# Layer one's experts: the second bias spread over the partitions at load and added by VectorE, instead of one-row products on TensorE

## The chip, the cores and the metric

One core of a Trainium2 chip runs the whole program. The metric is the device time of one execution in microseconds (us): the median of several runs, and for the profiled execution its own time. A profile holds one execution, with the start and duration of nearly every instruction of the five engines: PE (TensorE; its weight loads are listed apart as PEld), DVE (VectorE), ACT (ScalarE), POOL (GpSimd) and SP (SyncE), which here only issues DMA transfers.

## The reference, cut to what matters

The program is a model of four layers on an input of 8 sequences x 256 tokens x 128 channels. Each layer has an attention part and a feed-forward part. The change touches the feed-forward part of layer one only (`L0_ffn` in the reference, `l0_ffn` in the kernel): an attention, then four experts, of which each token takes the one with the largest logit.

```python
def moe(x, gate_w, gate_b, W1, b1, W2, b2):
    logits = x @ gate_w.T + gate_b
    top = jnp.argmax(logits, axis=-1)
    onehot = jax.nn.one_hot(top, N_EXPERTS, dtype=x.dtype)      # 4 experts
    h = jax.nn.relu(jnp.einsum('btd,ehd->bteh', x, W1) + b1)    # 128 -> 512
    y = jnp.einsum('bteh,edh->bted', h, W2) + b2                # 512 -> 128
    return jnp.einsum('bted,bte->btd', y, onehot)
...
h = _layernorm(x, axis=-1) * (1 + cb) + sb
x = x + gb * _L0_ffn_ref(h, ...)
```

`b2` has 4 x 128 numbers: one row of 128 for each expert. Everything is fp32.

## The kernel before

The kernel is written out by hand, engine by engine, with semaphores between them. Layer one runs as one pipeline over 16 places `m`: 0 to 7 are the attention of the 8 sequences, 8 to 15 (`is_ffn(m)`) the feed-forward parts of the same 8. A sequence is two tiles of 128 tokens (`T` = 2, index `t`). In iteration `m` the engines work on the scores of place `m+1`, the weighing of place `m`, the projections of place `m+3` and, where place `m-1` is a feed-forward part, on its experts. The order on each engine is that of the code.

An iteration on PE has two stretches. The *attention stretch* is six rounds `k` of scores, masks and weighing (L1376 to L1410), in which PE, DVE (a max over every round's scores, L2296), ACT (exponentials, L3377) and POOL take turns; the stacks that the scores read are put together by small transfers that SP issues (`expand_half`, L598), 24 for each place. The *expert stretch* follows (L1411 to L1423): `turn_post`, `rise` of experts 0 and 1, `choose_expert`, then `fall` 0, `rise` 2, `fall` 1, `rise` 3, `fall` 2, `fall` 3. `rise(m, e)` makes the four 128-wide pieces of an expert's hidden layer (L1345, ACT adds `b1` and takes the relu, L3429). `fall(m, e)` multiplies by `W2` (L1361, four products for each token tile, summed in PSUM) and adds `b2` with a fifth product (L1362), whose weight operand is one row of ones and whose moving operand is one row of 128 biases.

Every fp32 product stands in the profile as two records of PE, so that `fall` shows 8 records of L1361 and 2 of L1362 for a token tile.

DVE picks the expert of every token (`pick_expert`, L2208 to L2226, a mask `picks` of 0 and 1), then for each expert waits for `fall` and adds bank x mask to the sequence's rows in SBUF (`add_expert`, L2232, one instruction for each token tile), and at the end multiplies by the gate and adds to `x` (`finish_ffn`, L2238 and L2241). `fall` 2 and 3 write the PSUM banks of `fall` 0 and 1 and wait until `add_expert` has read these.

The weights of a part are one matrix of 128 rows in HBM, in which `b2` fills only row 0 (512 columns, the other rows are zeros). SP loads the matrix with one transfer (`load`, L651) into one of two regions of SBUF; PE waits for that of `l0_ffn` in `scale_of_ffn` (L1117), at the beginning of the program.

Of the kernel before, what the change touches and what calls it, by code (L numbers as in the profile page):

```python
# [9 lines left out]
ALU = mybir.AluOpType  # L10
# [3 lines left out]
P = 128  # L14
B, S, D = 8, 256, 128
T = S // P
# [12 lines left out]
E0, C0 = 4, 4  # L29
# [29 lines left out]
WEIGHED = PHASES[:-1]  # L59
# [28 lines left out]
def offsets(cols):  # L88
    at, out = 0, {}
    for name, n in cols:  # L90
        out[name] = (at, n)
        at += n
    return out, at
# [29 lines left out]
H_RING = 6  # L123
# [15 lines left out]
def is_ffn(m):  # L139
    return B <= m < 2 * B  # L140
# [11 lines left out]
def last_of(m):  # L152
    return 2 * B - 1 if m < 2 * B else 3 * B - 1
# [17 lines left out]
def adaln_program(nc, x_in, c_in, const_in, ali_in, weights_in, out):  # L171
    ctx = ExitStack()
    with ctx:
        def sb(name, shape, dt=F32):
            return ctx.enter_context(nc.sbuf_tensor(name, shape, dt))
# [8 lines left out]
        def once(name):  # L184
            return ctx.enter_context(nc.semaphore(name))
# [13 lines left out]
        places = {ph: offsets(COLUMNS[ph]) for ph in WEIGHED}  # L199
        region = [sb(f"weights{i}", [P, max(places[ph][1] for ph in WEIGHED[i::2])]) for i in range(2)]  # L200

        def W(ph, name, rows=P):
            at, n = places[ph][0][name]
            return region[WEIGHED.index(ph) % 2][0:rows, at:at + n]
# [3 lines left out]
        ones = sb("ones", [P, P])  # L208
# [42 lines left out]
        hid = sb("hid", [P, 2, C0, T * P])  # L251
# [107 lines left out]
        h_ring = tail[1][:, 0:H_RING * S].rearrange("p (i t d) -> p i t d", t=T, d=D)  # L359
# [66 lines left out]
        loaded = [once(f"weights_loaded_{ph}") for ph in WEIGHED]  # L426
# [161 lines left out]
        def there(n):  # L588

            return 0 <= n < N3  # L590
# [56 lines left out]
        def _(sp):  # L647
            sp.dma_start(x[:], x_in.rearrange("b (t p) d -> p (b t) d", p=P)).then_inc(x_loaded, 16)
            def load(i):
                n = DOWN_AT if WEIGHED[i] == "l1_ffn" else places[WEIGHED[i]][1]  # L650
                sp.dma_start(region[i % 2][:, 0:n], weights_in[WEIGHED[i]][:, 0:n]).then_inc(loaded[i], 16)  # L651

            load(0)
            sp.dma_start(silu_c[:], c_in).then_inc(c_loaded, 16)
# [6 lines left out]
            for i in range(HPG):  # L661
                at = 64 * i + STACK_ROWS
# [45 lines left out]
            for i, ph in enumerate(WEIGHED):  # L708
                if 1 <= i < len(WEIGHED) - 1:

                    sp.wait_ge(pass_done.sem, pass_done(ph, 0, 1))
                    if ph == "l1_ffn":
                        n = places[ph][1]
# [346 lines left out]
        def _(pe):  # L1060
            mm = nc.tensor.matmul
# [48 lines left out]
            def spread_mod(ph, j, to):  # L1110
                for b in range(B):
                    last = mm(to[:, b * D:(b + 1) * D], silu_n[:, b, :], W(ph, "wmod")[:, j * D:(j + 1) * D], start=True, stop=True)
                last.then_inc(mod_psum, 1)

            def scale_of_ffn(ph="l0_ffn"):

                pe.wait_ge(loaded[1], 16)  # L1117
                pe.wait_ge(mod_taken, 2)
                spread_mod(ph, 1, scored)

# [227 lines left out]
            def fall(m, e, ph="l0_ffn"):  # L1348
                pe.wait_ge(relu_done.sem, relu_done(m, 2 * e + 2))
                if e < 2:  # L1350
                    if m + 1 <= last_of(m):
                        pe.wait_ge(weighed_taken.sem, weighed_taken(m + 1, e + 1))
                    if is_ffn(m - 1):
                        pe.wait_ge(fall_used.sem, fall_used(m - 1, e + 3))
                else:
                    pe.wait_ge(fall_used.sem, fall_used(m, e - 1))
                for t in range(T):
                    o = pb[4 + e % 2][:, t * D:(t + 1) * D]
                    for c in range(C0):
                        at = (e * C0 + c) * D  # L1360
                        mm(o, hid[:, e % 2, c, t * P:(t + 1) * P], W(ph, "w2")[:, at:at + D], start=c == 0, stop=False)  # L1361
                    last = mm(o, ones[0:1, :], W(ph, "b2", 1)[:, e * D:(e + 1) * D], start=False, stop=True)  # L1362
                last.then_inc(fall_psum.sem, 1)

            def piped(ph):
# [535 lines left out]
        def _(dve):  # L1901
            V_ = nc.vector
# [197 lines left out]
            def link(ins):  # L2100
                linked[0] += 1
                ins.then_inc(link_dve, 1)

            def linkup():

                dve.wait_ge(link_dve, linked[0])
# [101 lines left out]
            picks = small[8][:, 0:T * E0].rearrange("p (t e) -> p t e", t=T)  # L2208

            def pick_expert(m, ph="l0_ffn"):  # L2210
# [14 lines left out]
                link(V_.tensor_tensor(picks, order, every_e, ALU.is_equal))  # L2225
                linkup()  # L2226

            def add_expert(m, e):
                h = h_ring[:, m % H_RING]
                dve.wait_ge(fall_psum.sem, fall_psum(m, e + 1))  # L2230
                for t in range(T):
                    last = V_.scalar_tensor_tensor(h[:, t, :], pb[4 + e % 2][:, t * D:(t + 1) * D], picks[:, t, e:e + 1], h[:, t, :], ALU.mult, ALU.add)  # L2232
                last.then_inc(fall_used.sem, 1)
                dve.wait_ge(fall_used.sem, fall_used(m, e + 1))
# [115 lines left out]
            def piped(ph):  # L2350
                first = RUNS[ph][0]
                if ph == "l2_attn":
                    dve.wait_ge(pass_done.sem, pass_done(ph, 0, 1))
                    V_.memset(stacks[0], 0.0).then_inc(stacks_clear, 1)
                    V_.memset(stacks[1], 0.0).then_inc(stacks_clear, 1)
                    V_.memset(ones_h, 1.0).then_inc(stacks_clear, 1)
                stats_piped(first)
                mod_piped(ph)
                stats_piped(first + 1)
                norm_piped(first)  # L2360
                stats_piped(first + 2)
                if ph == "l0_attn":
                    dve.wait_ge(ali_loaded, 16 * HPG * 2)
                    V_.tensor_copy(stacks[0].rearrange("p g side n -> p (g side n)"), staging).then_inc(stacks_clear, 1)
                intake_piped(first)
                norm_piped(first + 1)
                stats_piped(first + 3)
                gates_piped(gates_attn, MODS[ph] + 2, MODS[ph] + 2, scored)
                intake_piped(first + 1)
                norm_piped(first + 2)  # L2370
                stats_piped(first + 4)
                if ph == "l0_attn":
                    scale_of_ffn()
                intake_piped(first + 2)
                if ph == "l0_attn":
                    mod_ffn()
                for m, there in iterations(ph):
                    for k in range(NU):
                        if m in (3 * B - 1, 3 * B) and k in (0, 3):
                            (wide_norm_of if k else wide_stats_of)("l2_ffn", m - 3 * B + 1)  # L2380
                        if k == 1 and there(2) and is_ffn(m + 2):
                            keys_ffn(m + 2)
                        if k == 2 and there(-1):
                            tokens_piped(m - 1)
                        if m >= first and k == 3 and there(3):
                            if is_ffn(m + 3):
                                queries_ffn(m + 3)
                            else:
                                intake_piped(m + 3)
                        if k == 4 and there(-1):  # L2390
                            if is_ffn(m - 1):
                                post_stats(m - 1)
                            else:
                                result_piped(m - 1)
                        if k == 5 and there(1):
                            values_piped(m + 1)
                        if k == 5 and there(3) and is_ffn(m + 3):
                            latent_stats(m + 3)
                        if there(1):
                            max_piped(m + 1, k)  # L2400
                        if m >= first and k == 0 and there(3):
                            if is_ffn(m + 3):
                                rms_ffn(m + 3)
                            else:
                                norm_piped(m + 3)
                        if k == 3 and there(4) and is_ffn(m + 4):
                            norm_ffn(m + 4)
                        if k == 5 and there(3) and is_ffn(m + 3):
                            latent_norm(m + 3)
                        if k == 5 and there(-1) and is_ffn(m - 1):  # L2410
                            post_norm(m - 1)
                    if there(-1) and is_ffn(m - 1):
                        pick_expert(m - 1)
                        for e in range(E0):
                            add_expert(m - 1, e)
                        finish_ffn(m - 1)
                    if m >= first and there(5):
                        stats_piped(m + 5)
# [1448 lines left out]
```

## Time and profile before

| | us |
|---|---|
| median of 3 runs | 2461.11 |
| lowest and highest run | 2457.08, 2466.51 |
| profiled execution, its own time | 2468.3 |
| profiled execution, span from first to last instruction | 2466.3 |
| PE busy in the span | 1913.0 |
| DVE busy in the span | 1691.8 |

The span is what the rows of the trace add up to; 2.0 us lie around it. Busy time is a sum over the whole program. Layer one's pipeline takes the first 551 us of the span, the experts stand between 248 and 551 us.

### The profile page before, as it was taken

The numbers are of one execution on the slowest core, as the hardware profiler recorded it, in microseconds if no ns is written. First come the engines' busy times: TensorE is split into PE (matmuls) and PEld (weight loads), VectorE is DVE, ScalarE is ACT, GpSimd is POOL, SyncE is SP. The second block draws the span as 40 slices with busy tenths as digits, with TensorE's granted clock in tenths as the row PEclk, the third lists the DMA queues.
The fourth block names the chain that finished last, engine by engine and source line by source line (L and its number), as shares of the span: only waits on it lengthen the run. The fifth ranks groups of instructions, "written<-read, shape, count | busy, mean of one in ns | idle before, by whom it ended". The sixth has DMA issues, their size and how long they took to land.

```text
span 2466.3 us, 43977 instructions
## 1 busy us (share of the span) xinstructions
PE 1913.0 (78%) x14818; PEld 1352.5 (55%) x14818; DVE 1691.8 (69%) x5219; ACT 1136.3 (46%) x3338; POOL 902.0 (37%) x1198
## 2 busy tenths in 40 slices
PE   5888888985266676676669999999587679999955
PEld 3545666662155565564557566666354347677742
DVE  6777344326588888878976866666675458888647
ACT  2533333325777677777632222222154237666620
POOL 3433121005185467447543000000441127767711
PEclk8977889885555555555556999999698689999967
DMA  4111001002000000000001000000210100000000
GB/s 126 47 42 40 19 15 35 5 18 89 14 7 7 14 9 13 8 14 1 1 1 49 1 1 0 0 0 0 52 48 26 65 12 1 2 1 2 1 1 17
DMA packets 57809, 49.61 MB, mean 20 GB/s; under 512 B 7048, under 2 KB 55912, under 8 KB 57064
## 3 DMA queue, kind: packets, MB, share of 16 engines
q1 hardware_dynamic: 54548, 45.53, 5.8%
q8 instruction: 108, 1.77, 0.3%
q10 hardware_dynamic: 3040, 1.38, 0.2%
q14 instruction: 113, 0.93, 0.1%
HBM read 19.78 MB, written 1.05 MB: 8 GB/s over the span
## 4 chain that ended last, share of the span: by engine, by line
PE 38%; DVE 30%; SPq 10%; issue 8%; ACT 8%; POOL 6%; DMA 1%; DVEq 0%; ACTq 0%; POOLq 0%
SPq L598 9%; PE bank L1628 5%; PE bank L1620 5%; PE bank L1621 5%; DVE weights L2658 4%; ACT rope_c L3534 3%; ACT rope_s L3534 3%; PE bank L1345 3%; PE bank L1361 2%; PE bank L1712 2%; DVE small L2696 2%; DVE feat_o L2708 2%; DVE nmax L2585 1%; PE bank L1531 1%; PE bank L1761 1%
## 5 line engine op out<-in xcount | busy, mean ns | idle before, releaser
L1531 PE MATMUL bank<-V,probsT 128*128 128x9 f32 x1024 | 234.8, 362 | 79.1 <-ACT probsT L3545 79.1
L1531 PEld LDWEIGHTS bank<-V,probsT 128*128 128x128 f32 x1024 | 224.9, 327 | 116.1 <-ACT probsT L3545 96.7
L2296 DVE TENSOR_REDUCE nmax<-bank 128x4 f32<-128x1024 f32 x144 | 176.0, 1222 | 87.2 <-PE bank L1158 87.0
L3600 ACT ACTIVATE hid<-bank 128x512 f32<-128x512 f32 x144 | 85.7, 597 | 277.3 <-PE bank L1621 268.4
L1628 PEld LDWEIGHTS bank<-weights,hid 128*128 128x128 f32 x1152 | 149.9, 191 | 74.9 <-issue 64.1
L2903 DVE TENSOR_TENSOR hid<-hid,bank 128x512 f32<-128x512 f32 x144 | 98.6, 687 | 117.0 <-PE bank L1628 113.7
L3545 ACT ACTIVATE probsT<-bank 128x512 f32<-128x512 f32 x128 | 76.1, 597 | 179.5 <-PE bank L1518 177.1
L1628 PE MATMUL bank<-weights,hid 128*128 128x128 f32 x1152 | 151.9, 275 | 7.8 <-DVE O L2917 5.1
L1620 PE MATMUL bank<-O,weights 128*128 128x512 f32 x288 | 149.3, 600 | 0.9 <-DMA weights<-in_weights_l_ffn 0.9
L864 POOL MEMSET big<- 128x4096 bf16 x1 | 3.5, 3512 | 398.1 <-DVE x L2943 398.1
L1621 PE MATMUL bank<-O,weights 128*128 128x512 f32 x288 | 148.1, 596 | 0.0
L3634 ACT ACTIVATE big<-bank,nmax 128x256 f32<-128x256 f32 x256 | 119.7, 485 | 51.9 <-DVE nmax L3078 51.9
L754 POOL TENSOR_TENSOR big<-big,rinv 128x512 f32<-128x512 f32 x128 | 132.8, 1052 | 19.1 <-DVE rinv L3084 19.1
L2917 DVE SCALAR_TENSOR_TENSOR O<-bank,O 128x128 f32<-128x128 f32 x496 | 138.9, 342 | 0.0
L3377 ACT ACTIVATE feat_o<-bank 128x1024 f32<-128x1024 f32 x72 | 73.7, 1024 | 115.6 <-PE bank L1187 87.7
L3377 ACT ACTIVATE O<-bank 128x1024 f32<-128x1024 f32 x72 | 73.7, 1024 | 115.3 <-PE bank L1187 87.5
L2585 DVE TENSOR_REDUCE nmax<-bank 128x2 f32<-128x512 f32 x128 | 84.8, 682 | 35.0 <-PE bank L1505 35.0
L1505 PE MATMUL bank<-qT 48*128 48x256 bf16 x256 | 70.3, 402 | 45.7 <-ACT weights L3488 33.3
L3078 DVE TENSOR_REDUCE nmax<-bank 128x2 f32<-128x512 f32 x128 | 81.8, 680 | 24.5 <-PE bank L1712 24.5
L1621 PEld LDWEIGHTS bank<-O,weights 128*128 128x128 f32 x288 | 55.3, 192 | 69.9 <-issue 69.9
L3429 ACT ACTIVATE hid<-bank,weights 128x256 f32<-128x256 f32 x128 | 52.9, 471 | 80.2 <-PE bank L1345 80.1
L1518 PE MATMUL bank<-const,big 128*128 128x128 f32 x256 | 61.6, 420 | 36.2 <-POOL big L970 36.2
(677 smaller groups left out, 5404.0 us busy)
## 6 DMA issues: line engine op xcount, KB each, us to landing
qT<-parts SPq DMA_DIRECT2D x276, 32.0 KB
big<-V SPq DMA_DIRECT2D x192, 32.0 KB
big<-parts SPq DMA_DIRECT2D x180, 32.0 KB
weights<-in_weights_l_ffn SPq DMA_DIRECT2D x1, 4832.0 KB, 15.3
weights<-in_weights_l_attn SPq DMA_DIRECT2D x1, 3904.0 KB, 12.0
weights<-in_weights_l_ffn SPq DMA_DIRECT2D x1, 3628.0 KB, 14.6
qT<-V SPq DMA_DIRECT2D x96, 32.0 KB
weights<-in_weights_l_ffn SPq DMA_DIRECT2D x1, 2304.0 KB, 8.6
```

The costliest lines, as they stand in the source:

```text
L598: queue.dma_start(stacks[m % STACKS][to, u * HALF:(u + 1) * HALF], pair_of(m, at, *of)).then_inc(stack_in[u].sem, 16)
L754: nc.gpsimd.tensor_tensor(row, row, rinv[:, h % H, :].unsqueeze(2).to_broadcast([P, T, S]), ALU.mult).then_inc(scaled.sem, 1)
L1531: last = mm(pb[1][:, t * S + h * wide:t * S + (h + 1) * wide], probsT[:, h % 2, at:at + P], values_of(b, k)[:, h * wide:(h + 1) * wide], s ...
L1620: mm(pb[two][:], W(ph, "gate")[:, cols], pair_feat, start=True, stop=True)
L1621: mm(pb[two + 1][:], W(ph, "up")[:, cols], pair_feat, start=True, stop=True).then_inc(hid_psum.sem, 1)
L1628: last = mm(pb[6 + e % 2][:, j * D:(j + 1) * D], risen(e)[:, j * P:(j + 1) * P], W(ph, "down")[:, e * D:(e + 1) * D], start=True, stop=True)
L2296: V_.tensor_reduce(to, scored.rearrange("p (i a n) -> p i a n", i=HPG, n=n), AX.X, ALU.max, negate=True).then_inc(score_max.sem, 1)
L2585: V_.tensor_reduce(nmax[:, h, :], tiles(pb[2 + n % 3]), AX.X, ALU.max, negate=True).then_inc(max_ready.sem, 1)
L2917: last = V_.scalar_tensor_tensor(pair_sum[:, j, :], down[:, j, :], w, pair_sum[:, j, :], ALU.mult, ALU.add)
L3377: nc.scalar.activation(turned_probs[n % TURNS], turned_scores, ACT.Exp).then_inc(turned_exp.sem, 1)
L3534: nc.scalar.activation(signs[signed[0] % len(signs)], row_of(b, j), ACT.Sign, bias=tried[at][:, 0, j:j + 1], scale=-1.0, accum_out=tried[a ...
L3634: last = nc.scalar.activation(probs3[h % PROBS3][:, t * S:(t + 1) * S], pb[h % 4][:, t * S:(t + 1) * S], ACT.Exp, bias=nmax[:, h % H, t:t ...
```

## The change

The sum of five products in `fall` becomes one of four: L1362 goes. The biases are spread over all 128 partitions when the weights are loaded: the load of `l0_ffn` becomes three transfers, the columns ahead of `b2`, the columns behind it, and row 0 of the `b2` columns read once for each partition. DVE adds the bias times the mask in SBUF (`add_bias`, two instructions for each expert), for experts 0 and 1 ahead of `add_expert` 0, for experts 2 and 3 ahead of `add_expert` 1. Each `add_bias` ends with a wait for its own instructions (`linkup`).

```diff
             def load(i):
                 n = DOWN_AT if WEIGHED[i] == "l1_ffn" else places[WEIGHED[i]][1]
-                sp.dma_start(region[i % 2][:, 0:n], weights_in[WEIGHED[i]][:, 0:n]).then_inc(loaded[i], 16)
+                if WEIGHED[i] == "l0_ffn":
+                    at, n_bias = places["l0_ffn"][0]["b2"]
+                    end = at + n_bias
+                    sp.dma_start(region[1][:, 0:at], weights_in["l0_ffn"][:, 0:at]).then_inc(loaded[i], 16)
+                    sp.dma_start(region[1][:, end:n], weights_in["l0_ffn"][:, end:n]).then_inc(loaded[i], 16)
+                    sp.dma_start(region[1][:, at:end], weights_in["l0_ffn"][0:1, at:end].to_broadcast([P, n_bias])).then_inc(loaded[i], 16)
+                else:
+                    sp.dma_start(region[i % 2][:, 0:n], weights_in[WEIGHED[i]][:, 0:n]).then_inc(loaded[i], 16)
...
             def scale_of_ffn(ph="l0_ffn"):
-                pe.wait_ge(loaded[1], 16)
+                pe.wait_ge(loaded[1], 3 * 16)
...
                     for c in range(C0):
                         at = (e * C0 + c) * D
-                        mm(o, hid[:, e % 2, c, t * P:(t + 1) * P], W(ph, "w2")[:, at:at + D], start=c == 0, stop=False)
-                    last = mm(o, ones[0:1, :], W(ph, "b2", 1)[:, e * D:(e + 1) * D], start=False, stop=True)
+                        last = mm(o, hid[:, e % 2, c, t * P:(t + 1) * P], W(ph, "w2")[:, at:at + D], start=c == 0, stop=c == C0 - 1)
                 last.then_inc(fall_psum.sem, 1)
...
+            def add_bias(m, e, ph="l0_ffn"):
+                h = h_ring[:, m % H_RING]
+                for t in range(T):
+                    link(V_.scalar_tensor_tensor(h[:, t, :], W(ph, "b2")[:, e * D:(e + 1) * D], picks[:, t, e:e + 1], h[:, t, :], ALU.mult, ALU.add))
+                linkup()
...
                         for e in range(E0):
+                            if e < 2:
+                                add_bias(m - 1, 2 * e)
+                                add_bias(m - 1, 2 * e + 1)
                             add_expert(m - 1, e)
```

What stands on PE in the expert stretch of the first feed-forward place, from `choose_expert` to the first scores of the next iteration, before (a product is one row here, and equal rows are counted):

```order
L1329 MATMUL bank<-weights,next_feat 128x4 x2
L1361 MATMUL bank<-weights,hid 128x128 x4
L1362 MATMUL bank<-weights,ones 128x128
L1361 MATMUL bank<-weights,hid 128x128 x4
L1362 MATMUL bank<-weights,ones 128x128
L1345 MATMUL bank<-next_feat,weights 128x256 x4
```

And in the changed kernel, where `choose_expert` is L1336, `fall` L1368 and `rise` L1352:

```order
L1336 MATMUL bank<-weights,next_feat 128x4 x2
L1368 MATMUL bank<-weights,hid 128x128 x8
L1352 MATMUL bank<-next_feat,weights 128x256 x4
L1368 MATMUL bank<-weights,hid 128x128 x8
L1352 MATMUL bank<-next_feat,weights 128x256 x4
L1368 MATMUL bank<-weights,hid 128x128 x16
L1186 MATMUL bank<-big 128x256 x4
```

Eight one-row products go from each of the eight expert stretches; nothing else changes its place on PE. On DVE the same stretch, from the end of `pick_expert` to the next statistics, before:

```order
L2225 TENSOR_TENSOR small<-small 128x8
L2232 SCALAR_TENSOR_TENSOR weights<-bank,small,weights 128x128 x8
L2238 TENSOR_TENSOR weights<-weights 128x256
L2241 TENSOR_TENSOR x<-x,weights 128x256
L2112 BN_STATS stats<-x 128x6 x2
```

And in the changed kernel, where `add_bias` is L2237 and `add_expert` L2244:

```order
L2231 TENSOR_TENSOR small<-small 128x8
L2237 SCALAR_TENSOR_TENSOR weights<-weights,small 128x128 x4
L2244 SCALAR_TENSOR_TENSOR weights<-bank,small,weights 128x128 x2
L2237 SCALAR_TENSOR_TENSOR weights<-weights,small 128x128 x4
L2244 SCALAR_TENSOR_TENSOR weights<-bank,small,weights 128x128 x6
L2250 TENSOR_TENSOR weights<-weights 128x256
L2253 TENSOR_TENSOR x<-x,weights 128x256
L2118 BN_STATS stats<-x 128x6 x2
```

Eight additions in SBUF come in, four ahead of the first `add_expert` and four ahead of the second. On SP the queue of the program's first microseconds in the changed kernel, where the one transfer of 7256 columns has become three:

```order
L670 DMA big<-in_ali 6x4096 x2
L672 DMA big<-probs 3x8x256 x2
L654 DMA weights<-in_weights_l_ffn 128x5720
L655 DMA weights<-in_weights_l_ffn 128x1024
L656 DMA weights<-in_weights_l_ffn 128x512
L598 DMA qT<-parts 8x4x512
```

Their place in the queue is that of the single transfer, ahead of the first stack's transfers.

## Rows read from the trace of the kernel before

**Rows 1.** The page: span, busy time of each engine, granted clock in 40 slices

```profile
span 2466.3 us, 43977 instructions
PE 1913.0 (78%) x14818; PEld 1352.5 (55%) x14818; DVE 1691.8 (69%) x5219; ACT 1136.3 (46%) x3338; POOL 902.0 (37%) x1198
...
PEclk8977889885555555555556999999698689999967
```

**Rows 2.** Chain that ended last, 384 to 405 us: start, us, what

```profile
387.47 1.00 PE bank L1361 x8
388.47 0.41 PE bank L1362 x2
...
390.38 1.92 PE bank L1345 x8
...
399.84 1.09 PE bank L1361 x8
...
402.43 0.43 PE bank L1362 x2
...
402.95 0.62 DVE weights L2232 x2
```

**Rows 3.** The same chain, 254 to 552 us: shares, two of the longest pieces

```profile
by line: PE bank L1345 20.2%; PE bank L1361 19.3%; issue 16.6%; PE bank L1362 7.8%; PE bank L1207 3.4%; DVE nmax L2296 3.1%; DVE stats L2112 1.8%; PE bank L1315 1.5%; PE bank L1179 1.4%; DVE weights L2232 1.2%; ACT next_feat L3418 1.2%; PE 
...
293.76 3.78 PE bank L1345 x8
...
420.29 31.79 issue
```

**Rows 4.** Line L1362: duration in ns (min/median/max), starts, and who waited

```profile
L1362 PEld LDWEIGHTS bank<-weights,ones x128: 181/182/184, 256.2 to 549.4; 1*128 1x128 f32 x128
L1362 PE MATMUL bank<-weights,ones x128: 270/321/372, 256.2 to 549.5; 1*128 1x128 f32 x128
...
  DVE weights L2232: 99.7, 32
```

**Rows 5.** Line L1361: duration in ns (min/median/max), first and last start

```profile
L1361 PEld LDWEIGHTS bank<-weights,hid x512: 186/192/192, 255.1 to 549.0; 128*128 128x128 f32 x171
```

**Rows 6.** Timeline 388 to 397 us, ACT and DVE: start, us, idle before

```profile
388.50 0.17 DVE L2225 TENSOR_TENSOR small<-small 128x8 f32<-128x8 f32 x1
...
390.49 0.61 DVE L2232 SCALAR_TENSOR_TENSOR weights<-bank,small,weights 128x128 f32<-128x128 f32 x2 [1.82 <-PE bank L1362]
...
395.22 0.61 DVE L2232 SCALAR_TENSOR_TENSOR weights<-bank,small,weights 128x128 f32<-128x128 f32 x2 [4.12 <-PE bank L1362]
396.27 1.64 ACT L3429 ACTIVATE hid<-bank,weights 128x256 f32<-128x256 f32 x4 [3.09 <-PE bank L1345]
```

**Rows 7.** Groups of DVE by form: busy us, mean ns, idle before

```profile
L2232 DVE SCALAR_TENSOR_TENSOR weights<-bank,small,weights 128x128 f32<-128x128 f32 x64 | 19.5, 346 | 99.7 <-PE bank L1362 99.7
L1971 DVE SCALAR_TENSOR_TENSOR probs<-gate_sign,next_gate_b 128x128 f32<-128x128 f32 x8 | 2.3, 293 | 0.3
```

**Rows 8.** Timeline of SP, 340 to 420 us

```profile
370.98 18.08 SPq L598 DMA_DIRECT2D big<-parts  x24
```

**Rows 9.** Timeline, transfer page and chain of the first 30 us

```profile
8.71 0.42 SPq L651 DMA_DIRECT2D weights<-in_weights_l_ffn  x1
...
26.27 3.75 PE L1112 MATMUL bank<-weights,feat_o 128*128 128x128 f32 x16 [0.35 <-DVE weights L2267]
...
weights<-in_weights_l_ffn SPq DMA_DIRECT2D x1, 3628.0 KB, 14.6
...
out<-x SPq DMA_DIRECT2D x4, 256.0 KB, 2.3
...
24.00 0.74 SPq L598
```

**Rows 10.** Windows: PE, PEld, DVE, ACT, POOL busy, granted clock, DMA share, GB/s

```profile
294.00:300.00 6.00, 6.00 (x28) 4.15 (x29) 0.00 (x0) 2.06 (x5) 0.00 (x0) 0.51 0.13 38
300.00:318.00 18.00, 18.00 (x132) 15.22 (x131) 3.81 (x15) 5.24 (x13) 0.00 (x0) 1.00 0.00 1
...
384.00:404.00 20.00, 20.00 (x151) 16.65 (x151) 3.83 (x15) 6.48 (x16) 0.00 (x0) 0.97 0.05 15
```

## The prediction, made before the changed kernel ran

> **What bounds the kernel now.** I read the page first, then the line that goes, then the chain that ended last around it, and only then the neighbours on the other engines. The page [rows 1] says that PE is the busiest engine with 1913.0 of 2466.3 us, but a share over the whole program proves nothing for one stage. So the next question is who waits for the line that goes. The view of L1362 shows that DVE's `add_expert` (L2232) waited for it 32 times, 99.7 us in all [rows 4]: 8 sequences x 4 experts, every one. DVE is ahead of PE in the whole expert stretch. The view also gives the places: 128 records from 256.2 to 549.5 us, that is 64 products, 8 in each of 8 sequences.
>
> The chain that ended last then shows whether PE's time there sets the end. In the stretch of one sequence it runs through PE without a break: 1.00 us of L1361, 0.41 of L1362, again and again, with `rise` (1.92 us) between, up to the last bias product at 402.43, behind which stands DVE's last `add_expert` at 402.95 [rows 2]. From 254 to 552 us L1362 has 7.8% of the chain, 23.2 of 298 us [rows 3]. One piece of 31.79 us beginning at 420.29 is an "issue" with nothing in it; PE worked there on the experts of another sequence, so the chain lost its way in that sequence and 23.2 us belong to seven, 3.3 us each. PE is the bound in all eight expert stretches, and its windows say the same: 18.00 of 18.00 and 20.00 of 20.00 us busy [rows 10].
>
> **What goes.** 64 products. The price of one is what PE's order loses by it, start to start: 0.41 us (two records) [rows 2]. This is not its listed duration (a median of 321 ns a record [rows 4]), because durations overlap. It is also not the price of a normal product: eight records of L1361 take 1.09 us, 0.136 each, a bias record 0.205. 64 x 0.41 = 26.2 us; from the chain's shares, 8 x 3.3 = 26.5. I take 26.2.
>
> Whether a price of 0.41 really disappears is the one doubt on PE's side. The weight loads of the two kinds last nearly the same, 182 ns with one row and 192 ns with 128 rows [rows 4, 5]. The Trainium skill (TensorE: Matmul & The Clock Gate, section on LDWEIGHTS) says that a load of few rows takes as long as a full one, since the columns count; the loads of this trace agree. Read as a rule for the whole product, a bias product would cost like any other, and that is a rival below. The starts speak for 0.41: they are what follows it that is late, and without it the next group of L1361 can begin where the bias product began.
>
> **What is added on DVE.** 64 instructions on 128x128 in SBUF, one-to-one with the products. This form (bias, mask column and sum all in SBUF) isn't in the trace. The nearest rows: 293 ns for the same operation with SBUF operands and a constant, and 346 ns for the same with one operand in PSUM [rows 7]; a pair of the latter lasts 0.61 to 0.62 us [rows 2, 6]. So 18.8 to 22.1 us more of DVE's time. I take the upper end, 0.62 a pair. Are they hidden? In the sequence shown the mask is ready at 388.50 + 0.17 = 388.67 [rows 6]. Two pairs end at 389.91, with two short waits about 390.0. `fall` 0 loses two bias products, so `add_expert` 0 could begin at 390.49 - 0.82 = 389.67: it begins 0.3 us late and ends at about 390.6. That costs nothing, since its only customer is `fall` 2, which began two groups of 1.50 us ahead of 399.84 [rows 2], at 396.8, and begins after the change 4 x 0.41 sooner, at 395.2. The other two pairs, 1.24 us, stand ahead of `add_expert` 1, before which DVE sat idle for 4.12 us [rows 6], of which 0.8 us go because PE is sooner (only the two bias products of `fall` 1 lie between) and 0.3 us to the late start: 3.0 us remain for 1.24. From there to the last `add_expert`, which is the one on the chain, DVE has nothing new. Cost on the path 0; if the cover were gone, 32 pairs x 0.62 = 19.8 us.
>
> **What is late next in the stretch.** PE sooner means ACT's relu may become the wait. The tightest is expert 3: its relu runs 396.27 to 397.91 [rows 6] and moves ahead by 4 x 0.41 = 1.64 us with `rise` 3, to an end of 396.3. `fall` 3 stood at 399.84 [rows 2] and moves by 6 x 0.41 to 397.4. 1.1 us of room; no wait.
>
> **What is late next behind it.** The next attention stretch begins 8 x 0.41 = 3.3 us sooner. Its scores need the stack that SP puts together. SP's 24 transfers run 370.98 to 389.06 [rows 8] and land within 2 or 3 us (an estimate, from the 2.3 us in which a 256 KB transfer lands [rows 9]); they are wanted when the experts' last product ends at 402.9 [rows 2], after the change at 399.6. 8 us of room. SP, POOL and ACT all start each round from something that PE or DVE did after the expert stretch, so they move with it. At the last sequence DVE's `finish_ffn` releases layer two, which begins sooner by the same amount.
>
> **The load.** Two transfers more: two more issues of 0.42 us, and SP has nothing to do between 9.13 and 24.00 [rows 9]. The bytes are the same (3628 KB). Before, they landed at 8.71 + 14.6 = 23.3 us; the first reader on PE ran at 26.27 and was released by DVE, not by the load [rows 9]. A read of one row by 128 partitions isn't in the trace. Bounds: 0, as the bytes are no more, and 2.3 us, as for a transfer of 256 KB by itself, plus 0.84 for the issues; that is 26.4 at worst, 0.2 us past PE's start. Besides, from 24.00 us on the chain is SP's own queue [rows 9], not PE. I take 0.
>
> **Sum.** -26.2 on PE, 0 elsewhere. The profiled execution would go from 2468.3 to 2442.1 us (span 2466.3 to 2440.1). It stands 7.2 us above the median of the runs, 2461.1, so the median goes to 2434.9, -1.06%. A change of less than about 0.5% (12.3 us) couldn't be told from none; this one can.
>
> **Rivals.**
> *The bias product is worth less.* If removing it gives only a normal product's time, 2 x 0.136 = 0.27 us, since the rest of the 0.41 is something that the next group pays anyway, the gain is 64 x 0.27 = 17.5 us: 2443.6. For it: the equal loads. Against it: every start-to-start row. The Trainium skill's rule on loads (TensorE: Matmul & The Clock Gate, LDWEIGHTS), read for the whole product, would give this time.
> *DVE's additions land on the path.* All 32 pairs uncovered leave 26.2 - 19.8 = 6.4 us: 2454.7. Against it: the idle times [rows 6], with 3.0 us for 1.24 at one place and 4.6 us to spare at the other.
> *The head start is swallowed in the attention stretch*, by the stack's transfers or a wait that isn't tied to PE: 2461. It needs SP to end 8 us later than it does.
> *The granted clock (the one that ends on the other side).* `rise` 0 runs at the 1.2 GHz level (3.78 us for eight records at 293.76, clock 0.51 from 294 to 300), the rest of the stretch at 2.4 GHz (1.92 us, clock 1.00) [rows 2, 3, 10]. When the level rises isn't in the program's hands. If with the changed rhythm it rose only after `fall` 0, `rise` 2 and `fall` 1 (2.2 + 1.9 + 2.2 = 6.3 us at the high level), each sequence would lose 6.3 us: 50.4 - 26.2 = +24.2, 2485. It decides from 3.3 us a sequence on, and is measurable as slower from 4.8. Against it: before these products PE is as busy as ever, and they go from the middle of a stretch without an idle microsecond. In small doses (a group or two of 1.9 us won or lost in some sequences) it belongs to the range of the forecast.
>
> **How the numbers follow.** The forecast has 0.82, the cheaper product 0.09, DVE on the path 0.03, swallowed 0.04, the clock 0.02. The likeliest case is 2435. Its own spread: the runs before lie 4 to 5 us around their median, and two or three groups of 1.9 us of clock go either way, so 2426 to 2444. The range of 8 in 10 reaches on to the cheaper product with 3 us of spread: 2425 to 2447. Faster by over 0.5% (below 2448.8) are the forecast and the cheaper product: 0.91. Within 0.5%: DVE on the path and swallowed, 0.07. Slower: the clock, 0.02.
>
> **What would show it.** The timeline of a sequence: the two groups of `fall` are 1.09 us apart instead of 1.50, `fall` lasts 2.2 us instead of 3.0, and from the first `fall` to the next scores pass 12.1 us instead of 15.4. `add_bias` shows about 300 to 346 ns an instruction, and DVE's idle time ahead of `add_expert` falls from 99.7 us by some 20 (its own new work) and 26 (PE is sooner), to about 53; only at expert 0 is it nil. The three transfers land before 26.3 us and no wait for them stands on PE. From 254 us on the eight sequences come sooner by 3.3 us each, and behind 551 us everything has the old distances. Wrong would be: distances of 1.2 us instead of 1.09 between groups, a wait of PE for L2244 in `fall` 2, or windows of the expert stretch with a clock below 0.9.

## The result, and the profile after

| | before | changed |
|---|---|---|
| median, us | 2461.11 | 2424.7 |
| lowest and highest run | 2457.08, 2466.51 | 2418.24, 2427.16 |
| span of the profiled execution | 2466.3 | 2425.1 |
| PE busy | 1913.0 | 1862.2 |
| DVE busy | 1691.8 | 1713.8 |

The ratio is 0.9846, with a 95% interval of 0.9829 to 0.9863: the changed kernel is 36.4 us faster. In a second set of runs it was 2425.06 against 2460.64 us, a ratio of 0.9858 (0.9842 to 0.9874). The forecast was 2435 us, a gain of 26; the time lies 0.3 us below the range. The direction and the place were right, the gain was 1.4 times as large as forecast.

The page of the changed kernel:

```profile
span 2425.1 us, 43787 instructions
PE 1862.2 (77%) x14690; PEld 1323.2 (55%) x14690; DVE 1713.8 (71%) x5283; ACT 1136.0 (47%) x3338; POOL 902.6 (37%) x1198
...
PEclk7987889965555555555557999999698789999967
```

PE is busy for 50.8 us less, more than the 26 that the forecast took off it; DVE for 22.0 us more, the upper bound of the forecast (22.1). The mean granted clock over the program is the same (0.768 and 0.769).

The chain that ended last through the experts of one sequence (start, us, what), to be read beside [rows 2]; in this kernel `rise` is L1352, `choose_expert` L1336, `fall` L1368, `add_expert` L2244:

```profile
372.90 0.34 PE bank L1336 x4
373.24 1.89 PE bank L1368 x16
375.13 1.73 PE bank L1352 x8
376.86 1.78 PE bank L1368 x16
378.64 1.73 PE bank L1352 x8
380.37 3.58 PE bank L1368 x32
...
384.05 0.62 DVE weights L2244 x2
```

The products of two token tiles (16 records) take 1.78 us, 0.89 for the eight that took 1.09 before, and `rise` takes 1.73 us where it took 1.92 [rows 2]. So not only the bias products are gone; what stood behind them became faster. The chain of the kernel before has both times for the same eight records, 0.89 us behind `rise` and 1.09 behind a bias product:

```profile
392.31 0.89 PE bank L1361 x8
393.20 0.41 PE bank L1362 x2
393.61 1.09 PE bank L1361 x8
```

The stretch from the first `fall` to the beginning of `finish_ffn` shows the gain in one number. The windows view of that stretch, in the kernel before and in the changed one (us, then busy time and count of PE, PEld, DVE, ACT, POOL, granted clock, DMA share, GB/s):

```profile
387.33:403.60 16.27, 16.27 (x122) 13.67 (x121) 3.43 (x15) 3.97 (x10) 0.00 (x0) 1.00 0.03 9
```

```profile
373.10:384.69 11.59, 11.59 (x106) 10.80 (x105) 5.88 (x22) 3.96 (x10) 0.00 (x0) 1.00 0.03 8
```

PE is busy without a break in both, at the 2.4 GHz level (granted clock 1.00) in both; the stretch is 4.68 us shorter. It is as long in each of the eight sequences (16.26 to 16.27 before, 11.59 to 11.60 after), which makes 37.4 us. `rise` 0 and 1 ahead of it are 1.4 us longer in sum (51.0 against 52.4), and the attention stretches (from 228 us on) 4.1 us shorter (141.4 against 137.3). In both the granted clock wanders from sequence to sequence and from execution to execution (0.57 to 1.00). Over the thirteen kernels profiled here, whose code in these two places is the same, the sums were 135.2 to 141.4 us and 48.5 to 52.6 us. These differences are no effect of the change that a run here could show.

DVE and the additions in the same sequence (timeline):

```profile
374.27 0.17 DVE L2231 TENSOR_TENSOR small<-small 128x8 f32<-128x8 f32 x1
374.48 1.26 DVE L2237 SCALAR_TENSOR_TENSOR weights<-weights,small 128x128 f32<-128x128 f32 x4
375.78 0.61 DVE L2244 SCALAR_TENSOR_TENSOR weights<-bank,small,weights 128x128 f32<-128x128 f32 x2
376.42 1.26 DVE L2237 SCALAR_TENSOR_TENSOR weights<-weights,small 128x128 f32<-128x128 f32 x4
378.75 0.61 DVE L2244 SCALAR_TENSOR_TENSOR weights<-bank,small,weights 128x128 f32<-128x128 f32 x2 [1.06 <-PE bank L1368]
```

Beside [rows 6]: `add_expert` 0 finds its product ready and waits for nothing, `add_expert` 1 still waits 1.06 us for PE after four additions. The view of L2244 counts what is left of the 99.7 us of [rows 4]:

```profile
  PE bank L1368: 41.0, 24
```

24 waits instead of 32: the eight of expert 0 are gone, and nothing else is.

### The profile page after: what moved, and what is told of

The parts are those of the page before. It is cut to its first block, busy times and chain, and to the rows that moved or that the text cites. A ratio compares the mean times of both kernels' runs of the same rounds, so it can differ in the third digit from the quotient of the medians.

```text
span 2425.1 us, 43787 instructions
## 1 busy us (share of the span) xinstructions
PE 1862.2 (77%) x14690; PEld 1323.2 (55%) x14690; DVE 1713.8 (71%) x5283; ACT 1136.0 (47%) x3338; POOL 902.6 (37%) x1198
## 4 chain that ended last, share of the span: by engine, by line
PE 39%; DVE 31%; ACT 9%; issue 8%; SPq 6%; POOL 6%; ACTq 1%; DMA 0%; DVEq 0%; POOLq 0%
SPq L598 5%; PE bank L1634 5%; PE bank L1626 5%; PE bank L1627 5%; DVE weights L2673 4%; ACT rope_c L3549 3%; ACT rope_s L3549 3%; PE bank L1352 3%; PE bank L1718 2%; PE bank L1368 2%; DVE small L2711 2%; DVE feat_o L2723 2%; DVE nmax L2308 1%; DVE nmax L2600 1%; PE bank L1537 1%
## 6 DMA issues: line engine op xcount, KB each, us to landing
weights<-in_weights_l_ffn SPq DMA_DIRECT2D x1, 2860.0 KB, 12.1
```

## The experiments

The question was where the 11 us beyond the forecast's 26.2 came from. Theory A: few-row weight operands between full ones break the overlap of weight loads and products at both borders. Here a border is the place where a weight operand of few rows and one of 128 rows follow each other, and a full-row product is one whose operands have all 128 rows. Theory B: a fifth product simply costs 0.58 us (4.68 / 8). The figure to watch is the stretch from the first `fall` to `finish_ffn`, because in none of the kernels it varied by more than 0.02 us over the eight sequences.

**All 128 rows.** Rows 1 to 127 of the bias columns are zeros in HBM, so the product may read them all:

```diff
-                    last = mm(o, ones[0:1, :], W(ph, "b2", 1)[:, e * D:(e + 1) * D], start=False, stop=True)
+                    last = mm(o, ones[0:128, :], W(ph, "b2", 128)[:, e * D:(e + 1) * D], start=False, stop=True)
```

> The kernel before, with the fifth product of `fall` over all 128 rows instead of one (a weight operand of 128 x 128 ones; rows 1 to 127 of the bias columns are zeros, so the sum is the same). Theory A: it is the one-row weight operand between 128-row operands that is dear; it breaks the overlap of weight loads and products at both borders. In the trace of before the group of eight L1361 records takes 0.89 us behind `rise` and 1.09 us behind a bias product, and a record in the long groups of the changed kernel takes 0.112 us. Then a full-row bias product costs 2 x 0.112 = 0.22 us instead of 0.58, `fall` group and bias 1.12 us instead of 1.50, the stretch from the first `fall` to `finish_ffn` 11.59 + 8 x 0.22 = 13.4 us (before 16.27, changed kernel 11.59), and the whole program about 23 us below the kernel before (ratio 0.991). Theory B: a fifth product costs 0.58 us whatever its rows (a product of its own kind, with the ones as operand, or the larger sum): stretch 16.3 us, ratio 1.000.

2438.47 us, ratio 0.9897 (0.9876 to 0.9919), stretch 13.38 us. Theory A expected 13.4, Theory B 16.3: A holds, B falls. The bias products multiply 128 times as many numbers, and the kernel is 23 us faster than the kernel before. Its chain through `fall` 0, `rise` 2 and part of `fall` 1:

```profile
254.68 1.00 PE bank L1361 x8
255.68 0.22 PE bank L1362 x2
255.90 0.89 PE bank L1361 x8
256.80 0.22 PE bank L1362 x2
257.02 1.73 PE bank L1345 x8
258.75 0.89 PE bank L1361 x8
```

The bias product takes 0.22 us instead of 0.41, and what stands behind it 0.89 and 1.73 instead of 1.09 and 1.92 [rows 2].

The timelines show where the time is lost. First the kernel before, at one bias product: the load of its weight operand (PEld) and its product (PE) begin together, and so do the load and the product behind it.

```profile
388.40 0.29 PEld L1362 LDWEIGHTS bank<-weights,ones 1*128 1x128 f32 x2
388.40 0.48 PE L1362 MATMUL bank<-weights,ones 1*128 1x128 f32 x2
388.81 0.30 PEld L1361 LDWEIGHTS bank<-weights,hid 128*128 128x128 f32 x2
388.81 0.38 PE L1361 MATMUL bank<-weights,hid 128*128 128x128 f32 x1
```

Then the kernel with 128 rows, where each load begins 0.1 us ahead of its product, under the product before:

```profile
255.41 0.30 PEld L1362 LDWEIGHTS bank<-weights,ones 128*128 128x128 f32 x2
255.51 0.39 PE L1362 MATMUL bank<-weights,ones 128*128 128x128 f32 x2
255.63 0.64 PEld L1361 LDWEIGHTS bank<-weights,hid 128*128 128x128 f32 x5
255.74 0.61 PE L1361 MATMUL bank<-weights,hid 128*128 128x128 f32 x4
```

So the overlap that Theory A spoke of is broken at both borders. What keeps the load back there no view shows.

**64 rows.** The same edit with 64.

> As the kernel before, with the fifth product of `fall` over 64 rows (row 0 the biases, the others zeros). Theory A says that the loss is in any operand with fewer than 128 rows: stretch from the first `fall` to `finish_ffn` 16.3 us, ratio 1.000, as with one row. A variant of A, by which the loss grows with the missing rows, gives something between: about 14.8 us and 0.995. Theory B: 16.3 us and 1.000, so this run says something only if the full-row run is faster.

2459.81 us, ratio 0.9987 (0.9971 to 1.0003), stretch 16.28 us: no better than one row. The loss doesn't grow with the missing rows. The view of L1362 in this kernel, against that of one row [rows 4], and then of the kernel with 128 rows:

```profile
L1362 PEld LDWEIGHTS bank<-weights,ones x128: 182/184/186, 256.1 to 548.6; 64*128 64x128 f32 x128
L1362 PE MATMUL bank<-weights,ones x128: 272/322/373, 256.1 to 548.7; 64*128 64x128 f32 x128
```

```profile
L1362 PEld LDWEIGHTS bank<-weights,ones x128: 191/192/193, 255.4 to 521.9; 128*128 128x128 f32 x128
L1362 PE MATMUL bank<-weights,ones x128: 274/275/276, 255.5 to 522.0; 128*128 128x128 f32 x128
```

The durations of the loads hardly differ; what differs is the spread of the products, 272 to 373 ns against 274 to 276. One of the two records of a few-row product is 0.1 us longer, about half of what the way in costs (0.19 us, below).

**The two one-row products side by side.**

```diff
                 for t in range(T):
                     o = pb[4 + e % 2][:, t * D:(t + 1) * D]
+                    if t == 1:
+                        mm(o, ones[0:1, :], W(ph, "b2", 1)[:, e * D:(e + 1) * D], start=True, stop=False)
                     for c in range(C0):
                         at = (e * C0 + c) * D
-                        mm(o, hid[:, e % 2, c, t * P:(t + 1) * P], W(ph, "w2")[:, at:at + D], start=c == 0, stop=False)
-                    last = mm(o, ones[0:1, :], W(ph, "b2", 1)[:, e * D:(e + 1) * D], start=False, stop=True)
+                        last = mm(o, hid[:, e % 2, c, t * P:(t + 1) * P], W(ph, "w2")[:, at:at + D], start=c == 0 and t == 0, stop=c == C0 - 1 and t == 1)
+                    if t == 0:
+                        mm(o, ones[0:1, :], W(ph, "b2", 1)[:, e * D:(e + 1) * D], start=False, stop=True)
```

> As the kernel before, but the two one-row products of a `fall` stand next to each other: the first token tile's as its last, the second tile's as its first. Theory A (the loss is at the borders between one row and 128 rows): half the borders go. Two products together cost 4 x 0.112 + one pair of borders 0.36 = 0.81 us instead of 1.17, the stretch falls by 4 x 0.36 = 1.4 us to 14.8, the program by 11.5 us, ratio 0.9953. Theory B (the loss sits in the product itself): nothing changes, stretch 16.3 us, ratio 1.000.

2449.29 us, ratio 0.9939 (0.9919 to 0.9959), stretch 14.92 us. Theory A again: it expected 14.8, because it let four pairs of borders go, though the last way out lies behind the stretch and only seven borders go (7 x 0.193 = 1.35 us). The chain (here the first tile's product is L1365, the second's L1360, the others L1363):

```profile
255.88 1.00 PE bank L1363 x8
256.88 0.41 PE bank L1365 x2
257.29 0.22 PE bank L1360 x2
257.52 1.09 PE bank L1363 x8
258.60 1.73 PE bank L1345 x8
```

The second one-row product costs 0.22 us, the price of a full one. What is dear is not the one row but the change: 0.19 us on the way in (0.41 - 0.22), 0.20 on the way out (1.09 - 0.89). The three stretches give one price. The kernel before has 15 borders inside a stretch (8 in, 7 out, the last way out lies behind it): (16.27 - 13.38) / 15 = 0.193 us. Side by side has 8 borders: 13.38 + 8 x 0.193 = 14.92, as measured. A full-row bias product is (13.38 - 11.59) / 8 = 0.224 us.

**How many rows make a border.** Two runs with 127 and 96 rows, then two with 65 and 32, one profiled execution each; the edit is that of the first experiment with another number.

> As the kernel before, with the fifth product of `fall` over 127 rows (the last row of zeros left out; the sum is the same). If any difference in the number of rows makes the border (Theory A in its plain form), the stretch from the first `fall` to `finish_ffn` is 16.27 us as with 1 and 64 rows. If it is the groups of 32 rows that an operand touches, 127 rows touch all four like 128, and the stretch is 13.38 us.

> As the kernel before, with the fifth product of `fall` over 96 rows, three of the four groups of 32. Both readings of Theory A say 16.27 us for the stretch from the first `fall` to `finish_ffn`; 13.38 would mean that the border lies between 64 and 96 rows.

> As the kernel before, with the fifth product of `fall` over 65 rows. 64 rows gave 16.28 us from the first `fall` to `finish_ffn`, 96 and 127 rows 13.38. If the border lies where an operand no longer fits in 64 rows, this run shows 13.38; if it lies higher (three groups of 32 begun), it shows 13.38 as well, and only if all of 96 rows must be there 16.27.

> As the kernel before, with the fifth product of `fall` over 32 rows. Theory A in its present form (an operand of at most 64 rows beside one of more): 16.27 us from the first `fall` to `finish_ffn`, as with 1 and 64 rows.

| rows of the bias product | stretch, us | time, us |
|---|---|---|
| 1 | 16.27 | 2461.11 (median) |
| 32 | 16.26 to 16.27 | 2456.59 |
| 64 | 16.28 | 2459.81 (median) |
| 65 | 13.38 | 2438.89 |
| 96 | 13.38 | 2434.6 |
| 127 | 13.38 | 2438.44 |
| 128 | 13.38 | 2438.47 (median) |

The expectation for 96 rows was wrong in both its readings, and with it Theory A in its plain form, by which anything short of 128 rows is "few". The limit lies between 64 and 65 rows, and no step shows among 1, 32 and 64 rows or among 65, 96, 127 and 128. For these four kernels the stretch of the one profiled execution decides; it is the same in all eight sequences. The view of L1362 with 65 rows is that of 128:

```profile
L1362 PEld LDWEIGHTS bank<-weights,ones x128: 190/191/192, 256.3 to 522.7; 65*128 65x128 f32 x128
L1362 PE MATMUL bank<-weights,ones x128: 273/274/275, 256.4 to 522.8; 65*128 65x128 f32 x128
```

The Trainium skill says on another page than the one that the prediction weighed (TensorEngine Tiling (Array Packing), Key Properties and Overview) that the array can be split into tiles of 64 or 32 rows for a contract dimension of at most 64, and that changing this mode drains the engine. The limit of 64 rows agrees with these runs. But the kernel names no tiles, and no run shows that the array changes its mode here or that a drain is what passes in those 0.193 us; the runs show their number, where they fall, and that the load doesn't begin ahead of its product there.

**Without DVE's additions.** The second bias is left out.

```diff
-                            if e < 2:
-                                add_bias(m - 1, 2 * e)
-                                add_bias(m - 1, 2 * e + 1)
                             add_expert(m - 1, e)
```

> The changed kernel without `add_bias`: the second bias is left out altogether. Theory of the prediction: DVE's 64 additions are hidden behind PE, so the stretch from the first `fall` to `finish_ffn` stays at 11.6 us and the time is that of the changed kernel, ratio to before 0.9846 within its interval. Rival: they delay something after all (the late `add_expert` of expert 0 holds up `fall` 2): then this run is up to 8 x 1.2 = 10 us faster than the changed kernel, ratio 0.981.

2420.49 us, ratio 0.9829 (0.9809 to 0.9848), against 0.9846 (0.9829 to 0.9863) and 0.9858 (0.9842 to 0.9874) with the additions. The intervals overlap, but this one also takes in the rival's 0.981, so the times alone don't decide. The stretch does: the rival's late `fall` 2 would lengthen it, and it is 11.59 to 11.60 us in every sequence, as with the additions. They cost nothing there. Of the 5.6 us between this profiled execution and that of the changed kernel in its second set, 3.6 lie in `rise` 0 and 1 (48.6 us against 52.2), at clocks that wander in all kernels: two kernels without any addition had 52.6 and 48.5 us there (64 and 32 rows). The view of L2244 shows the cover that the additions took up, 62.3 us of waits against 41.0:

```profile
  PE bank L1368: 62.3, 32
```

**The additions behind the last `add_expert`.** `add_bias` for all four experts directly ahead of `finish_ffn`, where nothing covers it.

> The changed kernel with all four `add_bias` behind the last `add_expert`, where DVE's work stands on the chain. Eight additions and their waits take 2.52 us in the changed kernel's trace (1.26 + 1.26). If what hides them is only their place ahead of `fall`'s end, the stretch from the first `fall` to the first scores' max grows by 2.5 us in each of 8 sequences: 20 us above the changed kernel, about 2445, ratio to before 0.993. If DVE has slack in the following attention stretch as well, less than half of that is seen.

2443.29 us, ratio 0.9925 (0.9908 to 0.9942): 18.2 us above the changed kernel in the same set of runs. The stretch is 14.19 to 14.20 us, 2.6 longer, 20.8 in all. The timeline:

```profile
266.15 0.61 DVE L2244 SCALAR_TENSOR_TENSOR weights<-bank,small,weights 128x128 f32<-128x128 f32 x2 [1.18 <-PE bank L1368]
266.80 2.56 DVE L2237 SCALAR_TENSOR_TENSOR weights<-weights,small 128x128 f32<-128x128 f32 x8
269.40 0.42 DVE L2250 TENSOR_TENSOR weights<-weights 128x256 f32<-128x256 f32 x1
```

The same 64 instructions cost 0 or about 20 us by where they stand. Half of the change's gain hangs on that place.

**The load by itself.** The kernel before with the three transfers in place of the one, and nothing else.

> The kernel before with the load of `l0_ffn` as three transfers and everything else as it was. All theories of the prediction: nothing is gained or lost, ratio 1.000, the first stack's transfers of SP start at 24 us as before, and no wait of PE or DVE for the three transfers. Rival, from the changed kernel's trace, in which the sixth stack's transfers begin 2.9 us sooner (210.22 against 213.16) before any expert ran: the three transfers shorten the start, ratio 0.999.

2458.06 us, ratio 0.9992 (0.9981 to 1.0004), stretch 16.26 to 16.27 us. Neither a gain nor a loss that could be told from none. In the trace of the changed kernel the last of the three was issued at 9.60 us and took 14.1 us to land:

```profile
weights<-in_weights_l_ffn SPq DMA_DIRECT2D x1, 256.0 KB, 14.1
```

It landed at 23.7 us, 0.4 later than the single transfer of before [rows 9] and ahead of PE's first reader, which ran at 26.02 us in the changed kernel.

**The changed kernel once more.**

> The changed kernel once more, beside the two others on the same chip. Theory A (a one-row product between 128-row products costs 0.58 us: 0.22 of its own and 0.19 at each border): 64 x 0.58 = 37.4 us less than before, 2424, ratio 0.985, and the stretch from the first `fall` to `finish_ffn` 11.59 us in every sequence. Rival (the gain beyond 26 us is luck of the granted clock): a ratio nearer 0.989 in fresh runs.

2425.06 us, ratio 0.9858 (0.9842 to 0.9874), stretch 11.59 to 11.60. The gain beyond 26 us was no luck of one set: 0.989, the ratio of the forecast's gain, lies outside both intervals.

## Why the prediction was right or wrong

**PE bounds all eight expert stretches:** right. From the first `fall` to the last PE has no idle time in either kernel, in any of the eight sequences.

**The price of a bias product:** this is the step that failed, as a term of the sum that was mis-sized. The prediction said "The starts speak for 0.41: they are what follows it that is late, and without it the next group of L1361 can begin where the bias product began." The next group does begin there, but it isn't the same group: behind a bias product it took 1.09 us, behind another full product it takes 0.89. A bias product's 0.41 us were 0.22 of its own and 0.19 of border, and 0.19 more stood on the account of its successor. Its whole price inside a stretch was 8 x 0.224 + 15 x 0.193 = 4.69 us for a sequence, 37.5 for eight, against 26.2 forecast and 37.4 found. The rows for it were in the trace of before: in the chain of [rows 2], in lines that it left out, eight records of L1361 took 0.89 us where they stood behind `rise`. The prediction used the 1.09 as the natural pace of such a product ("0.136 each") and so never asked why two groups of one line differ. It even put `fall` 2 at 396.8, "two groups of 1.50 us ahead of 399.84", where the chain of before has it at 397.04: the missing 0.2 us are the way out that the group behind `rise` doesn't pay.

**The cheaper product, 17.5 us:** wrong, and to the other side: the products were worth more than 26.2 us, not less. It read the nearly equal durations of the loads (182 and 192 ns) as equal prices. The loads last as long; they begin later, and that is what costs.

**DVE's additions:** right in size (349 ns each and 1.26 us for four; forecast 346 and 1.24) and in place: hidden, nil idle at expert 0, no wait of `fall` 2. DVE's remaining idle time was 41.0 us, not 53, because PE was sooner by more than forecast (99.7 - 37.4 = 62.3 us, as the run without additions shows, and 21.3 for the additions). What they cost without cover was forecast at 19.8 us; the run with the additions last found 20.8 in the stretches and 18.2 in the time.

**What is late next:** right. ACT's relu stayed ahead of `fall` 3: with PE 1.4 us sooner per sequence than forecast, PE still is busy 11.59 of 11.59 us. The head start wasn't swallowed in the attention stretch.

**The load:** right, 0, shown by itself.

**The granted clock:** 1.00 from the first `fall` to `finish_ffn` in all eight sequences, before and after, so the rival in which the level rises later didn't happen. In `rise` 0 and 1 the clock was 0.60 to 0.74 in seven of the eight sequences and 1.00 in one, in both kernels; the prediction's test, a clock below 0.9 in windows of the expert stretch, would have spoken against the forecast there, in the kernel before as well as in the changed one.

**What was to show it:** the forecast said 1.09 us between two groups of `fall`; it is 0.89. It said 12.1 us from the first `fall` to the next scores; PE begins these at 383.88 in the changed kernel, 10.8 us after 373.10. The test named "distances of 1.2 us" as what would prove it wrong; it had no line for a distance below 1.09.

## What to carry to other kernels

In this kernel a product with at most 64 rows between products with 128 cost twice, 0.58 us in all instead of 0.22: by its own longer time and by that of its successor. So before you take an instruction's start-to-start time for what its removal gives, compare the line that follows it in two neighbourhoods of one trace: behind the instruction, and behind something else. Where such a product must stay, pad it with zero rows to 65 or more, or put all few-row products side by side; and give work that moves to another engine a place ahead of a wait, since the same 64 additions cost nothing there and about 20 us at the end of the stretch.

## What the runs showed of the hardware

At the 2.4 GHz level an fp32 product of 128 columns takes 0.22 us (two records, 0.112 each) from start to start, with 1 row beside another of 1 row or with 65 to 128 rows beside 128. A change between an operand of 1, 32 or 64 rows and one of 128 takes 0.193 us more (with 1 row 0.19 on the way in and 0.20 on the way out), and operands of 65, 96 and 127 rows can't be told from 128. At such a change the load of the weight operand begins together with its product, elsewhere in `fall` 0.1 us ahead of it. An fp32 sum with mask on VectorE takes 350 ns for 128 x 128 with all its operands in SBUF, no less than with one of them in PSUM (346 to 350 ns). A transfer that reads one row of HBM for 128 partitions, queued behind 3372 KB, landed 0.4 us later than the single transfer of before, and the program's time didn't change.
